# One step of a Mamba loop on four engines: the product with B next to its scan, the bias of dt as a matrix row, side work moved

## What is computed

```
for i in range(4):                                   # Mamba layers
    xz = einsum('bld,ed->ble', x, in_w);  xi, z = split(xz, 2)        # 256 + 256
    xc = silu(causal_conv4(xi, conv_w) + conv_b)
    dt, Bm, Cm = split(einsum('bld,ed->ble', xc, xp_w), [8, 24])      # 8 + 16 + 16
    delta = softplus(einsum('blr,dr->bld', dt, dt_w) + dt_b)
    h[t] = exp(delta[t] * A) * h[t-1] + (delta[t] * xc[t]) * Bm[t]    # 256 x 16 states
    y[t] = sum_s h[t] * Cm[t] + xc[t] * D
    x = einsum('bld,od->blo', y * silu(z), ow)
```

## Time and profile before

| what | us |
|---|---|
| three runs | 1728.37, 1730.82, 1734.09; median 1730.82 |
| the profiled execution, its own time | 1734.24 |
| its span (first to last instruction) | 1732.5 |
| stages before the Mamba loop's prologue | 0 to 748 |
| prologue, to the first scan | 748 to 787.9 |
| layer 0, four steps | 787.9 to 1034.2 |
| layers 1 to 3, twelve steps | 1034.2 to 1703.5 |
| last stage | 1703.5 to 1732.5 |
| busy in the span: PE, DVE, ACT, POOL | 1307.1, 1186.3, 1059.3, 1006.6 |

### The profile page before, as it was taken

The page is one execution under the profiler, slowest core; times in us unless marked ns, Lnnn a source line. Parts: engine busy times, 40 slices in busy tenths (PEclk is TensorE's granted clock), DMA queues, the critical chain, the costliest instruction groups (busy, mean ns, idle before and its releaser), DMA issues. The chain is left out here.

```text
span 1732.5 us, 23857 instructions
## 1 busy us (share of the span) xinstructions
PE 1307.1 (75%) x6419; PEld 641.4 (37%) x6419; DVE 1186.3 (68%) x1664; ACT 1059.3 (61%) x1846; POOL 1006.6 (58%) x1092
## 2 busy tenths in 40 slices
PE   5213388898931799967977888898888989898884
PEld 2113033333431455633433334343443434343431
DVE  4786367686766422215888788878888778877884
ACT  2210378797811122346877779877798778777782
POOL 1642310110152530054988978898899888888894
PEclk9655589998965799987998999999999999999998
DMA  1110231321201301442332234313341233323331
GB/s 53 37 37 11 91 109 64 100 79 61 91 26 39 134 12 33 122 108 76 75 79 71 48 73 112 79 38 83 87 112 52 62 77 94 82 55 78 87 92 54
DMA packets 86612, 124.39 MB, mean 72 GB/s; under 512 B 16946, under 2 KB 43440, under 8 KB 86112
## 3 DMA queue, kind: packets, MB, share of 16 engines
q1 hardware_dynamic: 79680, 104.65, 23.0%
q0 software_dynamic: 6816, 18.42, 3.5%
...
## 5 line engine op out<-in xcount | busy, mean ns | idle before, releaser
L1918 DVE TENSOR_TENSOR_SCAN hs<-decay,dbx 128x512 f32<-128x512 f32 x512 | 592.3, 1203 | 100.7 <-ACT decay L1810 91.5
L1535 POOL TENSOR_TENSOR hcm<-hs,Cc 128x512 f32<-128x512 f32 x384 | 488.8, 1286 | 110.3 <-DVE hs L1918 106.8
L1810 ACT ACTIVATE decay<-dtr,a_cur 128x512 f32<-128x512 f32 x512 | 355.6, 714 | 145.3 <-DVE hs L1918 136.4
L1650 PE MATMUL dbx<-ident_sb,scaled 128*128 128x128 f32 x1536 | 242.5, 289 | 98.6 <-DVE hs L1918 95.2
L1650 PEld LDWEIGHTS dbx<-ident_sb,scaled 128*128 128x128 f32 x1536 | 176.5, 145 | 314.3 <-DVE hs L1918 240.5
L1790 ACT ACTIVATE scaled<-duT,BT 128x256 f32<-128x256 f32 x528 | 236.0, 497 | 0.1
L1535 POOL TENSOR_TENSOR hck<-hs,Cc 128x512 f32<-128x512 f32 x128 | 168.0, 1312 | 19.1 <-PE y_bank L1667 11.8
L1647 PE MATMUL dbx<-du,spread_sb 128*128 128x512 f32 x256 | 154.9, 690 | 11.0 <-DVE hs L1918 11.0
L1908 DVE TENSOR_TENSOR dbx<-dbx,Bb 128x512 f32<-128x512 f32 x128 | 88.6, 692 | 78.4 <-PE dbx L1647 77.3
L1585 PE MATMUL slot<-XT,w_tap 128*128 128x512 f32 (+3 forms) x288 | 138.4, 608 | 4.5 <-PEq L1063 3.7
L758 ACT ACTIVATE ex<-tt 128x1024 f32<-128x1024 f32 x128 | 136.8, 1069 | 4.2 <-DVE tt L843 3.5
...
## 6 DMA issues: line engine op xcount, KB each, us to landing
...
```

The costliest lines, as they stand in the source:

```text
L1535: nc.gpsimd.tensor_tensor(dst, hs[:, p % HR, :], rows, ALU.mult).then_inc(s_hc, 1)
L1650: last = nc.tensor.transpose(dbx[p % 3][:, P * kk:P * kk + P], scaled[:, (b + k) % 2, kk, g, :, :].rearrange("p j c -> p (j c)"), ident[:, :])
L1810: nc.scalar.activation(dec[:, p % DR, :], dtr[:, b % 2, g, :], ACT.Exp, scale=a_cur[:, 4 * g + k:4 * g + k + 1]).then_inc(s_dec, 1)
L1918: nc.vector.tensor_tensor_scan(hs[:, p % HR, :], dec[:, p % DR, :], dbx[p % 3][:, :], 0.0, ALU.mult, ALU.add).then_inc(s_sc, 1)
```

## The change

1. **DVE**: `times_b` of unit 4i+3 stands directly before scan 4i+3. The gate of y moves from behind unit 4 to behind unit 7. dt is one `scalar_tensor_tensor`, max(slot, 0) + Ln.
2. **Bias of dt**: `w_dt` gets a 41st row with the bias, `dbc` a 41st row of ones (set once by DVE), so the dt product has the bias in it; Relu on ACT goes, Abs is one instruction over both halves. One more load per layer, in `load_pre`.
3. **ACT**: silu of z and the copy of duT are one instruction each over both halves (the three slots are one tensor); the scalings of k = 2, the output copy (from unit 25 to unit 16) and the copy of duT stand at other units.
4. **PE**: x_proj, the output product and the taps are cut into single products, and most side jobs stand behind other units.
5. **POOL**: 8 scalings behind weighings 28 to 31, 8 behind weighings 0 to 3 of the next step.
6. **Prologue**: xi of step 1 goes into the y banks, silu of xi of step 1 and of z of step 0 are done before the loop, `spread_dt` stands before the three `spread_c`, and DVE makes 8 of the 16 first scalings.

`hc_after` and `weighed` give the numbers that stood there before.

```diff
-            slot = [st5.enter_context(nc.psum_tensor(f"slot{i}", [P, 512], fp32)) for i in range(3)]
+            slots = st5.enter_context(nc.psum_tensor("slots", [P, 3, 512], fp32))
+            slot = [slots[:, i, :] for i in range(3)]
...
-            w_dt = sb(st5, "w_dt", [40, 256])
+            w_dt = sb(st5, "w_dt", [41, 256])
...
-            dbc = sb(st5, "dbc", [40, 512])
+            dbc = sb(st5, "dbc", [41, 512])
...
+                        sp.dma_start(w_dt[40:41, :].rearrange("o (h p) -> o h p", p=P), one(A["pre_cols"])[:, :, 2:4].rearrange("o p h -> o h p"), allow_slow_non_contiguous=True).then_inc(s_wpre, 16)
                         sp.dma_start(pre_cols[:, :], one(A["pre_cols"]).rearrange("o p e -> p (o e)")).then_inc(s_wpre, 16)
...
                     store_bc(0, 0)
                     spread_direct(0, 0)
+                    spread_dt(0, 0)
                     for k in range(DIRECT):
                         spread_c(0, 0, k)
-                    spread_dt(0, 0)
...
                         for p in range(UN):
                             weigh(l, b, p)
-                            if p == 0:
-                                scale_by_b(l, b, 15)
-                            if p >= 27:
-                                for x in range(3 * (p - 27), 3 * (p - 27) + 3):
+                            if p < 4:
+                                for x in (8 + 2 * p, 9 + 2 * p):
+                                    scale_by_b(l, b, x)
+                            if p >= 28:
+                                for x in (2 * (p - 28), 2 * (p - 28) + 1):
                                     scale_by_b(l, b + 1, x)
...
                     def dt_proj(l, n, h):
-                        if h == 0 and not first(l, n):
-                            pe.wait_ge(s_zs, at(l, n - 1, 2, 2))
                         pe.wait_ge(s_dbc, at(l, n, 1, 1))
+                        pe.wait_ge(s_one, 1)
...
-                            if v == 0:
-                                z(l, b, 0)
-                            if v == 2:
-                                z(l, b, 1)
-                            if v == 3:
-                                x_proj(l, n)
-                            if not first(l, b):
-                                if v == 4:
-                                    fold_quad(l, b - 1, 2, 1)
-                                if v == 5:
-                                    fold_quad(l, b - 1, DIRECT, 1)
-                                if v == 22:
-                                    out_proj(l, b - 1)
+                            if v in (0, 1) and not first(l, b):
+                                z(l, b, 1 - v)
+                            if v in (3, 4):
+                                x_proj(l, n, v - 3)
                             if v == 6:
                                 turn_b(l, n)
-                            if v in (7, 8):
-                                dt_proj(l, n, v - 7)
+                            if v in (8, 9):
+                                dt_proj(l, n, v - 8)
+                            if not first(l, b):
+                                if v == 5:
+                                    fold_quad(l, b - 1, 2, 1)
+                                if v == 7:
+                                    fold_quad(l, b - 1, DIRECT, 1)
+                                if v in (13, 14):
+                                    out_proj(l, b - 1, v - 13)
                             if v in (10, 11):
                                 start_y(l, b, v - 10)
                             if v == 12:
                                 fold_quad(l, b, 0, 0)
                             if v == 15:
                                 fold_quad(l, b, 0, 1)
-                            if v in (18, 19):
-                                turn_du(l, n, v - 18)
+                            if v in (16, 17):
+                                turn_du(l, n, v - 16)
                             if v == 20:
                                 fold_quad(l, b, 1, 0)
                             if v == 21:
                                 fold_quad(l, b, DIRECT, 0)
-                            if v in (24, 25, 27, 28):
-                                xi(l, b + 2, (v - 24) // 3, (0, 1) if v in (24, 27) else (2, 3))
+                            if v in (19, 22, 23, 24):
+                                tap = (19, 22, 23, 24).index(v)
+                                xi(l, b + 2, 0, (tap,))
+                            if v in (25, 27, 28, 29):
+                                tap = (25, 27, 28, 29).index(v)
+                                xi(l, b + 2, 1, (tap,))
                             if v == 26:
                                 fold_quad(l, b, 1, 1)
                             if v == 31:
                                 fold_quad(l, b, 2, 0)

...
+                    xi(0, 1, 0, every, y_bank)
                     for h in range(2):
                         turn_du(0, 0, h)
-                    for h in range(2):
-                        xi(0, 1, h, (0, 1, 2, 3))
+                    xi(0, 1, 1, every, y_bank)
+                    for h in (1, 0):
+                        z(0, 0, h)
                     pe.wait_ge(s_cst, 64)
...
                     def silu_z(l, b):
                         wait(act, s_op, at(l, b, 1, -1))
-                        for h in range(2):
-                            act.wait_ge(s_z, at(l, b, 2, h + 1))
-                            nc.scalar.activation(zs[:, b % 2, h, :], slot[2 if h == 0 else 0][:, :], ACT.Silu).then_inc(s_zs, 1)
+                        act.wait_ge(s_z, at(l, b, 2, 2))
+                        nc.scalar.activation(zs[:, b % 2, :, :], slots[:, 0:3:2, :], ACT.Silu).then_inc(s_zs, 1)
...
-                    def abs_and_relu(l, n, h):
-                        if h == 0:
-                            wait(act, s_dst, at(l, n, 16, 0))
-                            wait(act, s_dun, at(l, n, 2, 0))
-                        act.wait_ge(s_dtp, at(l, n, 2, h + 1))
-                        bias = pre_cols[:, 2 + h:3 + h]
-                        nc.scalar.activation(dt[:, h, :], slot[h][:, :], ACT.Abs, bias=bias).then_inc(s_ab, 1)
-                        act.wait_ge(s_ab, at(l, n, 3, h + 1))
-                        nc.scalar.activation(slot[h][:, :], slot[h][:, :], ACT.Relu, bias=bias).then_inc(s_rl, 1)
-
-                    def softplus(l, n):
-                        act.wait_ge(s_ab, at(l, n, 3, 2))
+                    def abs_dt(l, n):
+                        wait(act, s_dst, at(l, n, 16, 0))
+                        wait(act, s_dun, at(l, n, 2, 0))
+                        act.wait_ge(s_dtp, at(l, n, 2, 2))
+                        nc.scalar.activation(dt[:, :, :], slots[:, 0:2, :], ACT.Abs).then_inc(s_ab, 1)
+
+                    def exp_dt(l, n):
+                        act.wait_ge(s_ab, at(l, n, 2, 1))
                         nc.scalar.activation(dt[:, :, :], dt[:, :, :], ACT.Exp, scale=-1.0).then_inc(s_ab, 1)
-                        act.wait_ge(s_ab, at(l, n, 3, 3))
+
+                    def log_dt(l, n):
+                        act.wait_ge(s_ab, at(l, n, 2, 2))
                         nc.scalar.activation(dt[:, :, :], dt[:, :, :], ACT.Ln, bias=1.0).then_inc(s_ln, 1)
...
                         for w in range(UN):
                             decay(l, b, w)
-                            if w == 0:
+                            if w == 0 and not first(l, b):
                                 silu_xi(l, n)
                                 silu_z(l, b)
                                 act.preload_act_table_set("natural_log_exp_and_others")
-                            if b == 0 and w == 2:
+                            if b == 0 and w == 3:
                                 d_of_layer(l)
                             if w == 4:
                                 copy_dbc(l, n)
-                            if w == 8:
+                            if w == 7:
                                 copy_bt(l, n)
-                            if w in (10, 11):
-                                abs_and_relu(l, n, w - 10)
+                            if w == 10:
+                                abs_dt(l, n)
+                            if w == 11:
+                                exp_dt(l, n)
                             if w == 12:
-                                softplus(l, n)
-                            if 14 <= w < 22:
-                                for x in (2 * (w - 14), 2 * (w - 14) + 1):
+                                log_dt(l, n)
+                            if w in last_scales:
+                                for x in last_scales[w]:
                                     scale_by_b(l, b, 2, x)
-                            if w in (21, 22):
-                                copy_dut(l, n, w - 21)
-                            if 23 <= w < 31:
-                                for x in (2 * (w - 23), 2 * (w - 23) + 1):
+                            if w == 16 and not first(l, b):
```

(26 more changed lines are left out.)

130 lines of the change are left out of this document (71 added, 59 removed).

## The result

The changed kernel takes 1735.3 us (median of 20 runs, 1725.9 to 1741.3) against 1729.85 (20 runs, 1718.7 to 1734.1): ratio **1.0038, interval 1.0024 to 1.0052**. It is slower by 0.4%, where 1691 was forecast.

A forecast was written before the change was run, and what follows sets the result against it. DVE's chain of scans was taken to end each step, some 10 us of waits winnable. Layers 1 to 3 -24, layer 0 -6, prologue and step 0 -9: -39, profiled 1734.2 to 1695, median about 1691 us; range 1657 to 1722.

The forecast's parts named there:

- the one on GpSimd: GpSimd's weighings and scalings per step: cost 0, with 5 us left and eight buffers as cover; without that cover 2 us.
- The slower rival: ACT waits for both dt products before decay 11 and stays behind; up to +40 us, or 1746 in all; chance 0.10.
- Pairs, +1.0: DVE's eight products with B, each directly before the scan reading it: 0.13 us more per pair, +1.0 us a step.
- Rival 2: On DVE a dependent pair of product and scan costs nothing: 15 us less, 1676; chance 0.07.
- PE's waits, -2.6: DVE's waits for PE in steps of layers 1 to 3 fall from 5.2 to 2.6 us a step.
- ACT's block and small waits, -0.4: ACT's work between decay 0 and decay 1 gives -0.3 us a step, lessened small waits 0.1 us.
- Clock, rival 1: PE's clock stays up without the half-clock stretch: 1.2 us a step more go, 1670 in all; chance 0.17.
- Step, -2.0: Sum of the terms for one step of layers 1 to 3: -2.0 us, from 55.8 to 53.8.
- The three steps of layer 0: Three later steps of layer 0 have the same waits: -2 us each, -6.
- Prologue and step 0, -9: Before the loop and in step 0: dt stored 3.5 us earlier, 5.58 before scan 1 gone; -9 us.
- rival 5: ACT late before decay 11 makes the kernel slower: +40 us with all, 1746 with two thirds of 3.5; chance 0.10.
- Rival 3: DVE's waits for PE only move to later in the step: 1711, with pairs at 0.37 1722 or more; chance 0.20.

The follow-up runs named there:

- du_psum2: Changed kernel with dt made in its PSUM bank, where du reads it, and a DVE copy to SBUF for the store: 0.9858 of the kernel before.
- hold: Changed kernel with GpSimd waiting for scan 14 before weighing 12 (10 in the third step of a layer): 0.9754 of the kernel before.
- psum_pairs: Changed kernel with dt in PSUM and the taps of xi in pairs behind units 24, 25, 27, 28 again: 0.9926 of the kernel before.
- psum_timesb_back: Changed kernel with dt in PSUM and the product with B back one scan ahead: 0.9975 of the kernel before.
- again: The changed kernel run once more, unedited: 1.0007 of the kernel before.
- before_dtfirst: Kernel before with only dt's spreading put ahead of the three spreads of C in SP's prologue: 0.9971 of the kernel before.

## Why the prediction was wrong

The step that failed is the one on GpSimd: "0", because it was busy 47.89 of 56.10 us and eight buffers stood between it and DVE. It priced GpSimd as a supplier that could be late, and as a supplier it cost next to nothing: DVE waited for it once, 2.0 us. What GpSimd can do besides is keep DVE's one instruction with two SBUF inputs out, at times for as long as it runs without a pause. Measured: +2.8 us a step, some 33 in all, and the clock lost behind the stop. *du_psum2* and *hold* show it: with one input from PSUM, or with a pause, the long du are gone. A sign of it was readable before: the earlier trace rows and the shape of DVE's waits did not show it, since a blocked instruction counts as busy, but the durations did, three du of 4.0 us in one line with a median of 0.67, always in the steps with taps on GpSimd. The slower rival was another mechanism (ACT late before decay 11); of DVE's 47.1 us of waits for ACT all but a few tenths stand before scan 1, so ACT's lead held.

By the other terms:

- **Pairs, +1.0.** Right. The scan behind a product starts 0.03 after its end (1554.89 + 0.69, next at 1555.61), not 0.09 before; that is the median of all 96 pairs of layers 1 to 3. Rival 2, by which a pair is free, has this against it.
- **PE's waits, -2.6.** Right in size: 5.3 us a step became 2.6 (24.7 + 6.2 over twelve), in the changed trace with a lower clock than before. psum_pairs and psum_timesb_back show that both halves of it carry: by the ratios 0.7 and 1.3 us a step, each against the other part made.
- **ACT's block and small waits, -0.4.** Measured -0.6 (54.3 to 47.1 over twelve).
- **Clock, rival 1.** I gave it 0.17. With GpSimd out of the way the clock is 0.99 and a step 52.5 us in *hold* (51.5 by the estimate from *du_psum2*) against the 53.8 forecast; so it was the better forecast, hidden here by the stop of du.
- **Step, -2.0.** Take the added du time out of L1-3 and (675.7 - 33.4) / 12 = 53.5 us remain, where 53.8 was forecast. With *again* the same sum gives 53.9. The agreement is in part luck: without the stop the clock stays up as well, and a step takes 52.5 (*hold*). The three steps of layer 0 gave 1.4 instead of 6.
- **Prologue and step 0, -9.** Scan 1 starts 11.2 us earlier in the trace; 3.5 of it is SP's order (shown by before_dtfirst). That the rest is the moved silu was not run alone; the vanished 5.58 before scan 1 says so.
- **Two sums of the rivals** do not come out. With two thirds of the 3.5, rival 5 gives (2.3 + 1 - 1.2 + 2 - 2.6) x 15 = +23, so 1754 and not 1746. Rival 3 with pairs at 0.37 gives 1711 + 15 x 1.9 = 1740, far above the 1722 at which the range ends.
